# A three-stage audio tower kernel: new instruction orders, experts and gate output per 128 tokens, whole filter rows

## The chip, the cores and the metric

One NeuronCore of a Trainium2 chip runs the whole kernel. The metric is the device time in microseconds (us), lower is better. Engines: PE (TensorE), DVE (VectorE), ACT (ScalarE), POOL (GpSimd) and SP (SyncE, which here only issues DMAs). Each engine works through its own queue in order and meets the others through semaphores.

## The reference, cut to what matters

The input is 32 sequences of 750 rows of 256 channels. Each sequence becomes 3 segments of 128 tokens (every second row, zero-padded), that is T = 384 tokens. Per sequence:

```
h   = softmax(x x^T / 16) x                                 # per 128-token segment
z   = layernorm(h)
q,k,v = silu(causal_conv4(z W)) ; beta = sigmoid(z Wb)
o_delta = delta rule in chunks of 32 tokens, 4 heads of 64   # T = inv(I + A), state S over time
short, long = causal_conv3(v), causal_conv63(v)
w   = softmax(mlp([z, statistics of the four branches]))     # the gate, 4 weights per head
o   = rmsnorm(w0*short + w1*long + w2*o_delta + w3*v) Wo
h   = h + o
out = h + sum over the best 2 of 6 experts of layernorm(h)   # router, gelu MLPs 256 -> 128 -> 256
```

All is float32.

## The kernel before

Three stages run one after another; the loops are fully unrolled, each engine has its own hand-written list of calls, and the order of these lists is the schedule. NB = 32 sequences, BLK = 3 blocks of 128 tokens.

**First stage** (`first_phase`): attention, projections, the three-lag convolution of q, k and v, normalisation factors. Step i works on sequence a = i (attention), b = i-1 (projections and convolution taps), c = i-2 (short filter, k and v turned to tokens) and d = i-3 (masking of the k products). On DVE the 18 convolution taps of a sequence (`tap`, L737) are most of the work. `find_max` (L705) waits for PE's scores, `row_stats` (L716) for ACT's `divide_attn`, `variances` (L722) for the statistics just made. SP also writes one band of the long filter's Toeplitz tensor per issue (`expand`, 128 issues in all), 128 columns wide.

**Middle stage** (`second_phase`): the 63-tap filter as a matmul with Toeplitz tiles, 32 groups of 8 channels, four tile buffers. SP loads each group as two halves of 64 rows and 128 columns (64 issues, rows of 512 B), DVE clears the corner that the second half leaves empty, and PE does, per half group, four matmuls of 128 rows (L1050) and four of 64 rows (L1054) for what spills into the next 128-token block. Before groups 8, 16 and 24 stand three wide matmuls (`dense`, L1034). Meanwhile DVE inverts the 32x32 systems (`solve_column`, L1335 and L1338) and ACT stores the result of each head. The stage's last issues of SP are the first loads of the last stage.

**Last stage** (`third_phase`): step i works on n = i (products of q, k, kb; merging the inverses; state updates over the three blocks), it = i-1 (gate and mixture), e = i-2 (output projection, second norm, router, experts 0 to 2) and f = i-3 (experts 3 to 5). The names and lines that the prediction uses:

- PE: `products` L1468, `merge_a` to `merge_d` (L1477, L1488/L1491, L1499, L1507), `gate_out` L1587 (12 matmuls of the code, gate logits), `updates` L1538, `route` L1624, `state_update` L1547, `outputs` L1554, `kb_state` L1516, `q_state` L1524, `hidden` L1635, `expert_out` L1645 (all three blocks of an expert in one call).
- DVE: `mask` L1881 (masks the products; ACT's `copy_kk` then frees the bank), `gate_logits` L1943 to L1953, `gate_weights` L1958 to L1962, `weigh` L1968 and L1971, `state` L1917 (first) and L1919, routing L2017 to L2042, `remainder` L1908 (makes the right side R of the next `updates`), `add_expert` L2063.
- POOL: `VB` L2177, and, once the gate weights are there, L2182 and L2184 (two products of 768 columns per partition), and the powers of -1/2 (L2171, L2188).
- `solve_column` also runs here, on DVE: two columns in each of the steps 6 to 20, one to three in steps 0 to 5, after the second norm (`second_norm`, L2012) and before `gate_logits`.

A bank of PSUM that PE writes is read by DVE or ACT, and the next write waits for them. Most waits of PE in the last stage are of this kind.

## Time and profile before

| | us |
|---|---|
| median of 3 runs (lowest, highest) | 2646.76 (2645.16, 2649.2) |
| the profiled execution, its own time | 2644.78 |
| its span, first to last instruction | 2643.1 |
| PE, DVE, ACT, POOL busy | 2392.8, 1922.0, 1366.2, 562.4 |
| granted PE clock, mean | 0.966 |

The granted clock is given as a share of full speed: 1.00 is 2.4 GHz and 0.50 is 1.2 GHz. A row of the timeline has the start, the duration, engine, line, operation, what is written and read, a count of equal instructions in a row, and in brackets the engine's idle time before it with what ended it. An fp32 matmul of the code is two hardware matmuls, so x6 on L1645 are three matmuls of the code.

### The profile page before, as it was taken

To read this page: it belongs to the slowest core of one execution; us is meant where nothing else is said; L and a number is where in the kernel's file an instruction comes from. 1 tells how busy PE (TensorE), PEld (TensorE's weight loads), DVE (VectorE), ACT (ScalarE), POOL (GpSimd) and SP (SyncE) were. 2 spreads that over 40 slices of the span, in tenths; PEclk is the share of its full clock that TensorE was granted. 3 is DMA by queue.
4 is the path that set the end of the run, shared out by engine and by line. 5 is a ranking of instruction groups with operands and counts; after the bars stand their busy time and mean duration, and the time that the engine had idled before them with its cause. 6 is when DMAs were issued, how large, how long until landed. Compare 5 with 4: busy or idle time off the path is not lost.

```text
span 2643.1 us, 53850 instructions
## 1 busy us (share of the span) xinstructions
PE 2392.8 (91%) x21052; PEld 1789.0 (68%) x21052; DVE 1922.0 (73%) x5205; ACT 1366.2 (52%) x2633; POOL 562.4 (21%) x413
## 2 busy tenths in 40 slices
PE   5999999999698689999999999999999999999996
PEld 3666666666577567767777777777777777677764
DVE  3999999999684447676777677767775666657655
ACT  3888888887334144444444444444445444544442
POOL 1444444444200011111111111111111111111111
PEclk9999999999678589999999999999999999999999
DMA  2566666666889313221322122212322231223100
GB/s 85 202 218 224 214 212 225 216 214 214 209 218 282 110 58 112 67 70 64 108 100 70 64 94 90 70 64 76 108 70 88 70 114 65 70 70 111 64 19 19
DMA packets 253500, 318.25 MB, mean 120 GB/s; under 512 B 114496, under 2 KB 224032, under 8 KB 244544
## 3 DMA queue, kind: packets, MB, share of 16 engines
q1 hardware_dynamic: 248928, 292.78, 34.2%
q10 hardware_dynamic: 2304, 12.58, 1.4%
q0 software_dynamic: 2016, 9.44, 1.1%
q8 instruction: 169, 2.77, 0.4%
q14 instruction: 83, 0.68, 0.1%
HBM read 175.43 MB, written 156.11 MB: 125 GB/s over the span
## 4 chain that ended last, share of the span: by engine, by line
PE 41%; DVE 17%; ACT 6%; issue 3%; POOL 0%; DVEq 0%
PE bank L1645 7%; PE bank L1576 6%; PE bank L1635 5%; PE bank L1468 4%; PE bank L1587 4%; DVE DL L1977 3%; PE bank L1606 3%; ACT L1782 3%; DVE v_all L2063 3%; PE bank L1580 2%; PE bank L1499 2%; PE bank L1507 2%; PE bank L1554 1%; DVE e L2022 1%; ACT HE L1782 1%
## 5 line engine op out<-in xcount | busy, mean ns | idle before, releaser
L737 DVE SCALAR_TENSOR_TENSOR Y<-bank,convw,Y 128x383 f32<-128x383 f32 (+2 forms) x576 | 328.7, 603 | 4.5 <-ACT Y L626 3.2
L1645 PE MATMUL bank<-w2e,HE 128*128 128x256 f32 x1152 | 289.8, 388 | 12.1 <-DVE v_all L2063 9.2
L2063 DVE SCALAR_TENSOR_TENSOR v_all<-bank,we,v_all 128x256 f32<-128x256 f32 x576 | 242.8, 477 | 78.8 <-PE bank L1645 76.9
L1635 PE MATMUL bank<-v_all,w1e 128*128 128x384 f32 x768 | 285.9, 495 | 1.4 <-ACT HE L1782 1.4
L448 PE MATMUL bank<-pb,wqkv 128*128 128x384 f32 x768 | 275.3, 489 | 0.6 <-DVE Y L737 0.6
L1943 DVE TENSOR_TENSOR L<-bank,b2g 128x48 f32<-128x48 f32 x32 | 6.6, 207 | 344.0 <-PE bank L1587 344.0
L1645 PEld LDWEIGHTS bank<-w2e,HE 128*128 128x128 f32 x1152 | 208.1, 192 | 49.3 <-issue 16.6
L1576 PE MATMUL bank<-v_all,w1g 128*128 128x384 f32 x512 | 201.9, 518 | 0.4 <-ACT v_all L1774 0.4
L1782 ACT ACTIVATE HE<-bank 128x384 f32<-128x384 f32 x192 | 94.1, 490 | 194.8 <-PE bank L1635 194.1
L1765 ACT ACTIVATE v_all<-bank 128x192 f32<-128x192 f32 x192 | 60.1, 331 | 253.6 <-DVE v_all L1881 253.5
L2182 POOL TENSOR_TENSOR v_all<-v_all,WT 128x768 f32<-128x768 f32 x32 | 72.6, 2267 | 506.9 <-DVE WT L1962 506.9
L1635 PEld LDWEIGHTS bank<-v_all,w1e 128*128 128x128 f32 x768 | 134.1, 191 | 64.9 <-issue 9.6
L448 PEld LDWEIGHTS bank<-pb,wqkv 128*128 128x128 f32 x768 | 134.4, 191 | 61.4 <-issue 1.1
L2188 POOL TENSOR_TENSOR m<-m,minus_half_q 128x12 f32<-128x12 f32 x32 | 72.6, 2268 | 334.6 <-DVE m L1983 334.6
L626 ACT ACTIVATE Y<-bank,convw 128x384 f32<-128x384 f32 x192 | 111.5, 581 | 56.5 <-PE bank L448 54.1
L1757 ACT ACTIVATE first_stage<-bank 32x384 f32<-32x384 f32 (+1 forms) x192 | 89.0, 479 | 99.1 <-PE bank L1488 43.3
L1468 PE MATMUL bank<-v_all 64*128 64x256 f32 x768 | 115.1, 420 | 20.4 <-PEq L1009 14.4
L1554 PEld LDWEIGHTS bank<-W,v_all 128*128 128x128 f32 x768 | 98.4, 196 | 33.8 <-ACT W L1757 25.9
L1782 ACT ACT_TABLE_LOAD x93 | 119.3, 1283 | 1.7
L1554 PE MATMUL bank<-W,v_all 128*128 128x64 f32 x768 | 105.2, 281 | 15.1 <-ACT W L1757 15.1
L2171 POOL TENSOR_TENSOR b<-b,minus_half_q 128x3 f32<-128x3 f32 x32 | 27.1, 848 | 428.9 <-DVE b L2007 428.9
L1576 PEld LDWEIGHTS bank<-v_all,w1g 128*128 128x128 f32 x512 | 88.0, 191 | 42.8 <-issue 1.2
(213 smaller groups left out, 5440.9 us busy)
## 6 DMA issues: line engine op xcount, KB each, us to landing
packa<-pa SPq DMA_DIRECT2D x32, 1932.0 KB, 6.2
v_all<-packa SPq DMA_DIRECT2D x32, 1932.0 KB, 7.7
packb<-pb SPq DMA_DIRECT2D x32, 768.0 KB, 4.3
v_all<-packb SPq DMA_DIRECT2D x32, 768.0 KB, 7.0
toeplitz<-taps SPq DMA_DIRECT2D x128, 128.0 KB, 3.3
toep<-toeplitz SPq DMA_DIRECT2D x64, 256.0 KB, 7.1
packb<-fsk SPq DMA_DIRECT2D x32, 384.0 KB, 2.3
first_stage<-fl SPq DMA_DIRECT2D x32, 384.0 KB, 5.5
```

What stands on the lines that cost most here:

```text
L448: mm = pe.matmul(proj_bank[j][:, 0:T], wqkv[:, a, j * P:(j + 1) * P], xnT[:, a, :], start=(a == 0), stop=(a == HALF - 1), skip_group_check ...
L626: act.activation(Y[:, j, :], proj_bank[j][:, 0:T], ACT.Copy, scale=convw[:, j, CK - 1:CK])\
L737: dve.scalar_tensor_tensor(out=Y[:, j, lag:T], in0=proj_bank[j][:, 0:T - lag], scalar=convw[:, j, CK - 1 - lag:CK - lag], in1=Y[:, j, lag: ...
L1468: mm = pe.matmul(bank[odd][:, hh * 2 * P:(hh + 1) * 2 * P], kT[rows, hh, pair * P:(pair + 1) * P], qkb[rows, :, hh, pair * P:(pair + 1) * ...
L1554: mm = pe.matmul(bank[1][:, h * DH:(h + 1) * DH], ATM[:, even_heads_first(b, h), 0:P], W[:, h, :], start=(b == 0 and h == 0), stop=True, s ...
L1576: pe.matmul(mlp_bank[m][:, 0:T], w1g[:, a, m * P:(m + 1) * P], chans(pb[s], PX)[:, a, :], start=(a == 0), stop=False)
L1587: mm = pe.matmul(bank[4][:, b * P:(b + 1) * P], GH[:, m, b * P:(b + 1) * P], w2g[:, m, :].unsqueeze(1).broadcast_to([P, P // (4 * NH), 4 * ...
L1635: mm = pe.matmul(bank[6][:, 0:T], w1e[:, a, k, :], YT[s][:, a, :], start=(a == 0), stop=(a == HALF - 1))
L1645: mm = pe.matmul(expert_bank(b), HE[k % 2][:, b * P:(b + 1) * P], w2e[:, k, :], start=True, stop=True)
L1757: return act.activation(dst, src, ACT.Copy)
L1782: act.activation(HE[k % 2][:, :], bank[6][:, 0:T], ACT.Gelu_apprx_tanh).then_inc(he_ready.sem, 1)
L2063: dve.scalar_tensor_tensor(out=HA[s][:, b, :], in0=expert_bank(b), scalar=we[s][:, b, k:k + 1], in1=HA[s][:, b, :], op0=ALU.mult, op1=ALU. ...
```

## The change

- **Filter rows.** `toeplitz` is TW = 190 columns wide instead of 128. `expand` writes 190 columns, always from offset P-1-p. A group is loaded with one DMA of 128 whole rows (8 channels x 190 columns = 6080 B in a row), DVE's four clears of the corner and PE's wait for them go, and the second four matmuls take all 128 rows.
- **Experts per block.** `expert_out`, `add_expert`, `gate_out`, `input_stats`, the statistics of the delta branch and `second_norm` are called per block (or per pair of heads), so that other work can stand between. `eo_ready` counts 18 per sequence instead of 6. The third block's adds go on one by one; the first two share a bank and the first add waits for both.
- **Last stage, order.** Every engine has one `step(i)` as in the first stage, with another order. What is done is the same.
- **First stage, order.** PE, ACT, DVE and POOL lists are in another order, and so are the taps.

```diff
-            "toeplitz": nc.dram_tensor("toeplitz", [P, D, P], F32, kind="Internal").ap(),
+            "toeplitz": nc.dram_tensor("toeplitz", [P, D, TW], F32, kind="Internal").ap(),
...
-                    for half in range(2):
-                        rows = slice(half * DH, (half + 1) * DH)
-                        sp.dma_start(toep[it % NT][rows, :, half * (FL - 1):half * (FL - 1) + P],
-                                     dram["toeplitz"][rows, it * CG:(it + 1) * CG, :]).then_inc(toep_loaded[it % NT].sem, 16)
+                    sp.dma_start(toep[it % NT][:, :, :], dram["toeplitz"][:, it * CG:(it + 1) * CG, :])\
+                        .then_inc(toep_loaded[it % NT].sem, 16)
...
-                                mm = pe.matmul(acc[0:TW - P, o + NB:o + BLK * NB], toep[s][DH:P, ch, P:],
-                                               v_all[DH:P, it * CG + ch, 0:(BLK - 1) * NB],
+                                mm = pe.matmul(acc[0:TW - P, o + NB:o + BLK * NB], toep[s][:, ch, P:],
+                                               v_all[:, it * CG + ch, 0:(BLK - 1) * NB],
...
-                for s in range(NT):
-                    dve.memset(toep[s][DH:P, :, 0:FL - 1], 0.0).then_inc(setup, 1)
...
-                def expert_out(e, k):
+                def expert_out(e, k, b):
                     pe.wait_ge(*he_ready.now(e, k + 1))
...
+                    pe.wait_ge(*(acc_done.now(e, BLK * (k - 1) + max(b + 1, 2)) if k else acc_done.now(e - 1, BLK * (NE - 1) + max(b + 1, 2))))
+                    pe.matmul(expert_bank(b), HE[k % 2][:, b * P:(b + 1) * P], w2e[:, k, :], start=True, stop=True)\
+                        .then_inc(eo_ready.sem, 1)
...
+                def add_expert(e, k, b):
+                    s = e % 2
                     if k == 0:
                         dve.wait_ge(*we_step.now(e, 4))
...
+                    dve.wait_ge(*eo_ready.now(e, BLK * k + max(b + 1, 2)))
...
# DVE, last stage, around the masks
+                    if 0 <= n < NB:
+                        mask(n, 3)
+                        solve_columns(n)
                         mask(n, 4)
                         mask(n, 5)
...
# DVE, first stage, the end of a step
+                    if 0 <= a < NB:
                         row_stats(a, 0)
...
                         row_stats(a, 1)
...
                         row_stats(a, 2)
-                        variances(a)
                     if 0 <= c < NB:
                         copy_kbT(c)
-                    if 0 <= b < NB:
+                    if 0 <= a < NB:
+                        variances(a)
...
+                        tap(b, 3, 3)
                         tap(b, 4, 1)
+                    if 0 <= a < NB:
+                        normalise(a, 0)
+                        normalise(a, 1)
```

**Place 1: DVE in the last stage, from the gate weights to the remainder.** `m` stands for the small tiles m12, s12 and r12, `c` for cmp and eqs, `e` and `g` for the router's small tiles; first_stage is where the state S lies. Before:

```order
L1962 TENSOR_TENSOR WT<-WT,m 128x48
L1968 TENSOR_TENSOR DL<-DL,WT 128x768
L1917 COPY first_stage<-bank 64x2x64 x2
L2017 TENSOR_TENSOR c<-e,anchors 128x108
L2020 TENSOR_REDUCE e<-c 128x18
L2022 SCALAR_TENSOR_TENSOR e<-e,rclip 128x18
L2029 TENSOR_TENSOR c<-e 128x108
L2030 TENSOR_TENSOR c<-e 128x108
L2031 TENSOR_REDUCE g<-e 128x3
L2033 TENSOR_TENSOR c<-c,before_e 128x108
L2035 TENSOR_TENSOR e<-e,g 128x18
```

After:

```order
L1966 TENSOR_TENSOR WT<-WT,m 128x48
L2020 TENSOR_TENSOR c<-e,anchors 128x108
L2023 TENSOR_REDUCE e<-c 128x18
L2025 SCALAR_TENSOR_TENSOR e<-e,rclip 128x18
L1972 TENSOR_TENSOR DL<-DL,WT 128x768
L2033 TENSOR_TENSOR c<-e 128x108
L2034 TENSOR_TENSOR c<-e 128x108
L2035 TENSOR_REDUCE g<-e 128x3
L2037 TENSOR_TENSOR c<-c,before_e 128x108
L2039 TENSOR_TENSOR e<-e,g 128x18
L1922 COPY first_stage<-bank 64x2x64 x2
```

The copy of the first state, second after the gate weights before, now stands behind the eight router instructions.

**Place 2: PE in the last stage, from the gate output to the second block's updates.** Before:

```order
L1587 MATMUL bank<-w2g,v_all 128x128 x12
L1538 MATMUL bank<-VB,first_stage 128x128 x3
L1538 MATMUL bank<-VB,first_stage 128x64
L1645 MATMUL bank<-w2e,HE 128x256 x3
L1624 MATMUL bank<-router,v_all 128x126 x6
L1547 MATMUL bank<-W,v_all 128x128 x2
L1635 MATMUL bank<-v_all,w1e 128x384 x2
L1554 MATMUL bank<-W,v_all 128x64 x4
L1635 MATMUL bank<-v_all,w1e 128x384 x2
L1516 MATMUL bank<-first_stage,v_all 128x128 x2
L1645 MATMUL bank<-w2e,HE 128x256 x3
L1538 MATMUL bank<-R,first_stage 128x128 x3
```

After:

```order
L1565 MATMUL bank<-w2g,v_all 128x128 x12
L1605 MATMUL bank<-router,v_all 128x126 x6
L1516 MATMUL bank<-VB,first_stage 128x128 x3
L1516 MATMUL bank<-VB,first_stage 128x64
L1616 MATMUL bank<-v_all,w1e 128x384 x2
L1525 MATMUL bank<-W,v_all 128x128 x2
L1532 MATMUL bank<-W,v_all 128x64 x4
L1622 MATMUL bank<-w2e,HE 128x256
L1492 MATMUL bank<-first_stage,v_all 128x128 x2
L1616 MATMUL bank<-v_all,w1e 128x384 x2
L1622 MATMUL bank<-w2e,HE 128x256
L1516 MATMUL bank<-R,first_stage 128x128 x3
```

The reader of the first state (L1516 before, L1492 after) had two `hidden` and one whole `expert_out` ahead of it since the gate output, and has one `hidden` and one block of `expert_out` now; a `hidden` and a block follow it, ahead of the updates that need R.

**Place 3: DVE in the last stage, around the solve columns** (step of columns 15 and 16 after, 11 and 12 before). Before:

```order
L2012 TENSOR_SCALAR v_all<-v_all,bmv,b 128x256 x3
L1335 TENSOR_TENSOR prod<-X 128x660
L1338 TENSOR_TENSOR X<-X,prod 128x3x11x20
L1335 TENSOR_TENSOR prod<-X 128x684
L1338 TENSOR_TENSOR X<-X,prod 128x3x12x19
L1943 TENSOR_TENSOR L<-bank,b2g 128x48
```

After:

```order
L1886 TENSOR_TENSOR v_all<-bank,upper 128x2x128
L1332 TENSOR_TENSOR prod<-X 128x720
L1335 TENSOR_TENSOR X<-X,prod 128x3x15x16
L1332 TENSOR_TENSOR prod<-X 128x720
L1335 TENSOR_TENSOR X<-X,prod 128x3x16x15
L1886 TENSOR_TENSOR v_all<-bank,upper 128x2x128 x2
```

The columns have moved from behind the second norm to between the fourth mask and the last two.

## Rows read from the trace of the kernel before

**Rows 1.** By stretch: length, PE, PEld, DVE, ACT, POOL busy, PEclk, DMA share, GB/s.
```profile
400.00:419.80 19.80, 18.27 (x215) 13.08 (x214) 19.26 (x52) 16.14 (x36) 8.73 (x8) 1.00 0.63 218
697.00:867.00 170.00, 145.85 (x1042) 125.05 (x1042) 110.15 (x168) 60.51 (x75) 5.92 (x11) 0.75 0.96 246
703.80:748.00 44.20, 44.20 (x222) 38.07 (x223) 38.31 (x54) 11.73 (x14) 3.23 (x6) 0.50 0.82 187
973.50:2520.00 1546.50, 1464.61 (x11986) 1101.05 (x11986) 1072.60 (x3082) 716.16 (x1305) 245.94 (x144) 1.00 0.24 81
```
**Rows 2.** Waits of PE in 973.5 to 2520: total, times, longest.
```profile
PE bank L1538 <- DVE R L1908: 30.1, 29, 1.1
PE bank L1516 <- DVE first_stage L1919: 22.8, 29, 0.8
```
**Rows 3.** Timeline of PE, one step of the last stage.
```profile
1732.51 1.00 PE L1538 MATMUL bank<-VB,first_stage 128*128 128x128 f32 x8
1733.35 1.51 PE L1645 MATMUL bank<-w2e,HE 128*128 128x256 f32 x6
1734.70 1.50 PE L1624 MATMUL bank<-router,v_all 128*128 128x126 f32 x12
...
1738.61 1.51 PE L1635 MATMUL bank<-v_all,w1e 128*128 128x384 f32 x4
...
1740.40 1.46 PE L1645 MATMUL bank<-w2e,HE 128*128 128x256 f32 x6
1742.93 1.08 PE L1538 MATMUL bank<-R,first_stage 128*128 128x128 f32 x8 [1.07 <-DVE R L1908]
```
**Rows 4.** Timeline of DVE, the same step.
```profile
1732.71 0.21 DVE L1943 TENSOR_TENSOR L<-bank,b2g 128x48 f32<-128x48 f32 x1 [8.46 <-PE bank L1587]
...
1736.08 0.20 DVE L1958 TENSOR_REDUCE m<-WT 128x12 f32<-128x48 f32 x1
...
1736.82 0.96 DVE L1968 TENSOR_TENSOR DL<-DL,WT 128x768 f32<-128x768 f32 x1
1737.69 0.58 DVE L1917 COPY first_stage<-bank 64x128 f32<-64x128 f32 x2
1738.31 0.95 DVE L2017 TENSOR_TENSOR c<-e,anchors 128x108 f32<-128x108 f32 x1
...
1739.59 1.05 DVE L2022 SCALAR_TENSOR_TENSOR e<-e,rclip 128x18 f32<-128x18 f32 x1
1740.68 0.27 DVE L2029 TENSOR_TENSOR c<-e 128x108 f32<-128x108 f32 x1
...
1741.55 0.27 DVE L2038 TENSOR_TENSOR c<-c 128x108 f32<-128x108 f32 x1
```
**Rows 5.** Timeline of POOL, the same step.
```profile
1736.86 2.27 POOL L2182 TENSOR_TENSOR v_all<-v_all,WT 128x768 f32<-128x768 f32 x1 [14.91 <-DVE WT L1962]
1739.09 1.52 POOL L2184 TENSOR_TENSOR v_all<-v_all,WT 128x768 f32<-128x768 f32 x1
```
**Rows 6.** One line's instructions: ns shortest/median/longest, first and last start.
```profile
L2022 DVE SCALAR_TENSOR_TENSOR e<-e,rclip x32: 178/1053/1057, 992.2 to 2617.1; 128x18 f32<-128x18 f32 x32
```
**Rows 7.** Timeline of DVE, the second of two solve columns.
```profile
1562.46 0.91 DVE L1335 TENSOR_TENSOR prod<-X 128x720 f32<-128x720 f32 x1
```
**Rows 8.** DMA queues in 697 to 867: packets, MB, share of 16 engines.
```profile
q1 hardware_dynamic: 40143, 20.53, 59.7%
q10 hardware_dynamic: 2304, 12.58, 21.2%
```
**Rows 9.** Timeline of DVE, first stage.
```profile
402.29 0.56 DVE L705 TENSOR_REDUCE s<-bank 128x3 f32<-128x384 f32 x1 [0.17 <-PE bank L417]
...
410.03 0.31 DVE L722 BATCH_NORM_AGGREGATE mv<-st 128x2 f32<-128x6 f32 x3
```
**Rows 10.** Timeline of PE near the end, after an idle stretch.
```profile
2611.06 0.85 PE L1615 MATMUL bank<-ident,v_all 128*128 128x128 f32 x6 [2.50 <-DVE v_all L2012]
2611.74 2.63 PE L1645 MATMUL bank<-w2e,HE 128*128 128x256 f32 x6
```

More of the change, by code:

```diff
@@ new lines, in step @@
+                    if 0 <= n < NB:
+                        updates(n, n % 2, 0)
+                    if 0 <= e < NB:
+                        hidden(e, e % 2, 0)
+                    if 0 <= n < NB:
+                        state_update(n, n % 2, 0)
+                        outputs(n, 0)
+                    if 0 <= f < NB:
+                        expert_out(f, 5, 2)
+                    if 0 <= n < NB:
+                        kb_state(n, n % 2, 1)
+                    if 0 <= e < NB:
+                        hidden(e, e % 2, 1)
+                        expert_out(e, 0, 0)
@@ L1754, in _ @@
+                for i in range(NB + 3):
+                    step(i)
             @block.scalar
@@ L1872, in _ @@
-                body(it=NB - 1, e=NB - 2, f=NB - 3, s=1)
-                body(e=NB - 1, f=NB - 2, s=0)
-                body(f=NB - 1, s=1)
+                for i in range(NB + 3):
+                    step(i)
             @block.vector
@@ L2099, in body @@
[L2099 to L2109 removed]
+                    if 0 <= e < NB:
+                        residual(e, e % 2)
@@ L2200 @@
+                for i in range(NB + 2):
+                    step(i)
 _ATTN = ["Wq", "Wk", "Wv", "Wb", "conv_q_w", "conv_k_w", "conv_v_w", "fir_short_w", "fir_long_w", "mlp_w1", "mlp_b1",
```

832 lines of the change are left out of this document (425 added, 407 removed).

## Prediction, made before the changed kernel was run

> **What bounds the kernel now.** I read the busy time by stretch first [rows 1]. In the first stage DVE is busy 19.26 of 19.80 us, a whole step: DVE sets the pace there. In the middle stage (697 to 867) the DMA engines are busy for 0.96 of the time and PE's granted clock is 0.75; from 703.8 to 748 it is 0.50, and there PE is busy throughout while the DMA share is 0.82, so in that part PE is the bound and elsewhere DMA is. In the last stage PE is busy 1464.6 of 1546.5 us at clock 1.00; over its 29 steps of 53.4 us that leaves 81.9 / 29 = 2.8 us idle a step. The waits of PE say where [rows 2]: the right side R (1.1 a step) and the state S (0.8), both from DVE; the other 0.9 is two copies by ACT. The gain of an order lies in these 2.8 us, since no order takes away work.
>
> **Last stage, steady steps.** A wait costs more than its idle time: six matmuls of `expert_out` take 1.35 us to the next start (1733.35 to 1734.70) and 2.53 (1740.40 to 1742.93) with the 1.07 us wait behind them [rows 3], so about 0.1 more. Four waits are 2.8 + 4 x 0.15 = 3.4 us. Splitting `expert_out` adds no matmul. In the new PE order a block or a `hidden` stands in each of the four places, so these waits go. What is late next? I followed the new order from the end of `gate_out` at 1732.51, with the durations of before.
>
> PE reaches `kb_state` (it needs the first new state) after `route`, `state_update`, `hidden` and `outputs`, together 3.91 (1734.70 to 1738.61), `updates` 0.84 (1732.51 to 1733.35) and one block of `expert_out` 0.45 (a third of 1.35) [rows 3]: at 1737.7.
>
> DVE starts the gate logits at 1732.71; four operations of 0.24 and ACT's exp of the same 48 columns, taken as one more (an estimate), end at 1733.94; the weights take 0.74 (1736.08 to 1736.82) [rows 4]: 1734.68. Before, `weigh` and the copy of the state followed at once. Now the router's three operations stand first. Here the trace shows something that the order does not: L2022 works on 18 columns and lasts 1.05 us in the median but 0.18 at its shortest [rows 6], and the long ones end with POOL's second product: 1739.59 + 1.05 = 1740.64 against 1739.09 + 1.52 = 1740.61 [rows 4, 5]. L2017, 0.95 us, ends just past the first product's end, 1739.13, while L2029 on the same 108 columns takes 0.27. So a DVE operation with two inputs in SBUF stands still while POOL reads for its product, and POOL's product in turn ends 1.35 us after the DVE operation that got in first: 1739.13 - 1737.78 behind L1968, 1740.61 - 1739.26 behind L2017 [rows 4, 5].
>
> In the new order: L2017's operation gets in first (as L1968 did, 0.04 us ahead of POOL), 0.27, to 1734.95; POOL's first product ends 1.35 later, 1736.30; the operation of L2022 waits for it and ends at 1736.35; the second product ends 1.35 later, 1737.70; `weigh`, 0.96, two inputs in SBUF, waits for that, and is let in some 0.1 before its end: 1738.5; the ranking, 0.87 (1740.68 to 1741.55), 1739.4; the two state copies, 0.58, 1740.0. PE starts `kb_state` at 1740.1 instead of 1737.7: one wait of 2.4 us in the place of four that cost 3.4. Behind it, followed call by call in the same way, R, the second state and the experts' sums come 0.5 us or more ahead of PE. 29 x (3.4 - 2.4) = 29 us saved. With nothing standing still the copies would be ready at 1734.95 + 0.33 + 0.2 + 0.9 + 0.87 + 0.58 = 1737.8, and the wait 0.2: 93 us saved. I take the first, since all but the last of the 32 executions of L2022 fit it.
>
> The Trainium skill, page "SBUF — State Buffer", section "Who interferes with whom", has the rule: a VectorE instruction with two SBUF inputs and a GpSimd instruction that reads SBUF exclude each other for the whole instruction. It speaks against this order, which puts two such operations and then `weigh` where POOL works. By it the saving is the 29 us, without it 93; the 1.05 against 0.18 us above agree with it.
>
> **Last stage, the solve columns.** Before, they run while DVE waits for the gate output, with 8.46 us of idle left behind them [rows 4]: they cost nothing. Now they stand ahead of the last two masks, and `merge_a` on PE waits for ACT's copies behind these masks: queued behind it are the gate's matmuls and all the rest of the step. An operation on 720 columns takes 0.91 [rows 7], a pair of columns up to 4 x 0.94 = 3.8 us. The margin is bounded by nothing below and by 3.8 above; I estimate 1.8 (about 1.4 in which the fifth mask would wait for PE's third products anyway, and 0.4 of PE's `hidden`). By size (0.2 us an operation and 1 us for each 960 columns) the pairs of steps 6 to 20 take 1.35, 2.0, 2.55, 3.0, 3.35, 3.6, 3.75, 3.8 and back; what is over 1.8 adds to 17 us lost (0 to 43 at the ends). Steps 0 to 2 have two or three columns and little else to do: 4 us more lost, less if PE's wait for the residual in step 2 goes.
>
> **Middle stage.** Queue 10 stores 6144 B in a row per partition: 21.2% of 16 x 170 us for 12.58 MB, 46 engine-us per MB. Queue 1: 59.7% is 1624 engine-us for 20.53 MB; 58 half groups of 256 KB are 15.2 MB, the other 5.3 MB at 46 take 244, so 512 B rows cost 1380 / 15.2 = 91 per MB [rows 8]. The new group is 778 KB in pieces of 6080 B, nearest to queue 10: 29 x 0.778 = 22.6 MB x 46 = 1040. That saves 340 / 16 = 21 us where DMA is the bound, which it is in 126 of 170 us [rows 1]: 16, and I take 14, since a faster feed leaves PE's half-clock part as it is. The ends are 22 and, if the rows cost what 512 B rows cost, 42 lost. The four cleared corners and PE's wait for them cost nothing before. The first stage writes half as much again of Toeplitz rows; its DMA share of 0.63 [rows 1] covers that.
>
> The Trainium skill, page "DMA: Bandwidth & Descriptors", table "Specifications", gives 512 B as the transfer from which the line rate is reached. By that rule the new rows bring only the larger volume: this is a rival below. The 91 against 46 above speak against it.
>
> **First stage.** DVE is the bound, so only its own gaps count. Where nothing is waited for, an operation starts 0.08 us before the last one's end. `find_max` starts 0.17 after it, 0.25 lost; it now has three more DVE operations ahead of it since the copy of x, and PE makes the scores half a projection earlier. `variances` starts at 410.03, 0.10 behind the statistics that it needs [rows 9], 0.18 lost; a copy now stands between. Two taps of one tile in a row (0.11) are parted. That is 0.54 a step; the three `row_stats` in a row may wait 0.1 for ACT. 31 x 0.45 = 14 us saved, with 20 saved and 10 lost as ends.
>
> **Sum**, against the profiled execution's 2644.8: -29 + 17 + 4 - 14 - 14 = -36, 2609; the median of the runs is 2 above: **2611 us**.
>
> **Rivals.** *No standing still* (the copy of the state comes in time): 64 us more saved, 2547. For it: the new order fits exactly if each operation lasts its undisturbed time. Against it: rows 5 and 6. 15%. *The clock falls*, the one that ends slower: at 2611.06 PE had been idle for 2.50 us, and the next `expert_out`, six matmuls, took 2.63 instead of 1.46 [rows 3, 10]: 1.2 us, about 2 with what follows. The new wait is 2.4 us long, in one piece, before `hidden`; the four of before are at most 1.1. If the clock falls behind it in every step, 58 us more: 2669. It turns the result from 18 steps on (36 / 2). Against it: 2.4 is the shorter idle time. 15%. *Wide rows bring only bytes*: 7.4 MB more at 46 and DMA-bound for 126 of 170 us is 16 us lost where I count 14 won: 2641. 5%. *The middle stage is held by PE at half clock*: nothing won there, 2625. 10%. *The first stage gains a wait* of 1 us a step, since all its lists are new: 31 more and no 14: 2656. 5%.
>
> **How the numbers follow.** The forecast has 50%, with 2580 to 2640 as its own range from the ends of the margin (1 to 3 us) and of the middle stage. The range 2565 to 2655 leaves out most of the first rival and half of the second, about 2 in 10. A change under 0.2% (5.3 us) can't be told from none. Faster by more (below 2641.5): the forecast, the first and fourth rival, half of the third and part of the clock rival, 0.82; within: 0.06; slower: 0.12.
>
> **What the profile after would show.** PE waiting at `kb_state` for DVE's first state, 2.2 to 2.4 us a step, no wait at `updates` for R; L2025 (L2022 before) and `weigh` long, ending with POOL's products; in steps 7 to 19 PE waiting before `merge_a` for ACT, up to 2 us, and periods that rise and fall with the columns: 52.4 without columns, up to 54.4 with them; the toep queue's engine time down by a fifth and the middle stage 10 to 20 us shorter; DVE's period in the first stage 19.3. It would be wrong most of all if PE's clock drops behind the new wait, or if the state copies come in time.

## The result and the profile after

| | before | after |
|---|---|---|
| median (lowest to highest), us | 2646.57 (2645.16 to 2649.2, 4 runs) | 2534.92 (2528.05 to 2547.43, 4 runs) |
| profiled execution, its span | 2643.1 | 2526.3 |
| granted PE clock, mean | 0.966 | 0.978 |

The ratio is 0.9582, with a 95% interval from 0.9536 to 0.9628. The forecast was 2611 us with a range of 2565 to 2655: the direction was right, the gain is three times the size forecast, and the time lies outside the range. A second series gave 2537.97 against 2647.26, 0.9591 (0.9569 to 0.9613).

I cut the spans at the same places of the program and compared each part with its term in the sum. The profiled execution of the kernel after was the fastest of its four: the spans differ by 116.8 us, the medians by 111.7.

| part | before, us | after, us | difference | forecast |
|---|---|---|---|---|
| start to the first dense matmul | 689.9 | 671.8 | -18.1 | -14 |
| middle stage, to the first product of the last stage | 177.4 | 140.8 | -36.6 | -14 |
| filling, products of sequences 0 to 2 | 139.8 | 138.1 | -1.7 | +4 |
| 28 steady steps (products 3 to 31) | 1494.5 | 1446.9 | -47.6 | -12 (-29 and +17) |
| from the last products to the end | 141.5 | 128.7 | -12.8 | none |

The sum is -116.8. Two terms were far too small, and one was missing. Below, the period is the time from the first product of one sequence to that of the next. The stretches of the profile after, with the columns of [rows 1] (length, PE, PEld, DVE, ACT, POOL busy, PEclk, DMA share, GB/s): a step of the first stage, the middle stage, the steady part of the last.

```profile
382.00:401.27 19.27, 18.04 (x214) 12.98 (x214) 19.10 (x51) 15.95 (x36) 8.72 (x8) 1.00 0.72 237
671.80:812.60 140.80, 119.74 (x1052) 101.83 (x1053) 110.35 (x175) 60.89 (x75) 7.86 (x15) 0.94 0.96 365
927.00:2402.00 1475.00, 1414.84 (x11676) 1079.98 (x11677) 1055.81 (x3035) 713.67 (x1284) 239.66 (x143) 1.00 0.25 84
```

The DMA share of the middle stage is 0.96 as before, but it moves 365 GB/s where it moved 246, and PE's clock is 0.94 where it was 0.75 [rows 1]; it falls only at 798.8 us, behind the last filter matmul (795.3). PE's waits in 973.5 to 2380, against the list in [rows 2]:

```profile
PE bank L1492 <- DVE first_stage L1922: 50.1, 27, 1.9
```

Of the four waits a step one is left, at `kb_state` (L1492), for the first state copy: the place that the forecast named. PE, DVE and POOL around it (against [rows 3 to 5]):

```profile
1864.48 1.50 PE L1605 MATMUL bank<-router,v_all 128*128 128x126 f32 x12
...
1869.29 0.65 PE L1622 MATMUL bank<-w2e,HE 128*128 128x256 f32 x2
1871.80 0.71 PE L1492 MATMUL bank<-first_stage,v_all 128*128 128x128 f32 x4 [1.86 <-DVE first_stage L1922]
```
```profile
1866.42 0.21 DVE L1966 TENSOR_TENSOR WT<-WT,m 128x48 f32<-128x48 f32 x1
1866.55 0.27 DVE L2020 TENSOR_TENSOR c<-e,anchors 128x108 f32<-128x108 f32 x1
1866.85 0.27 DVE L2023 TENSOR_REDUCE e<-c 128x18 f32<-128x108 f32 x1
1867.15 1.09 DVE L2025 SCALAR_TENSOR_TENSOR e<-e,rclip 128x18 f32<-128x18 f32 x1
1868.16 0.94 DVE L1972 TENSOR_TENSOR DL<-DL,WT 128x768 f32<-128x768 f32 x1
1869.03 1.56 DVE L2033 TENSOR_TENSOR c<-e 128x108 f32<-128x108 f32 x1
...
1871.16 0.58 DVE L1922 COPY first_stage<-bank 64x128 f32<-64x128 f32 x2
```
```profile
1866.71 1.50 POOL L2231 TENSOR_TENSOR v_all<-v_all,WT 128x768 f32<-128x768 f32 x1 [11.84 <-DVE WT L1966]
1868.17 2.30 POOL L2236 TENSOR_TENSOR v_all<-v_all,WT 128x768 f32<-128x768 f32 x1
```

Read them together. L2025, 18 columns and two inputs, lasts 1.09 us and ends with POOL's first product; L2023, which has one input, takes its 0.27 us while that product runs. `weigh` (L1972) starts at 1868.16, 0.01 us ahead of POOL's second product, and runs its 0.94 undisturbed; the product ends 1.4 us after it, at 1870.47, and L2033, 108 columns, stands for 1.56 us until then.

### The profile page after: what moved, and what is told of

It reads as the page before. It is cut to its first block, busy times and chain, and to the rows that moved or that the text cites. A ratio compares the mean times of both kernels' runs of the same rounds, so it can differ in the third digit from the quotient of the medians.

```text
span 2526.3 us, 54742 instructions
## 1 busy us (share of the span) xinstructions
PE 2317.6 (92%) x21052; PEld 1750.0 (69%) x21052; DVE 1909.3 (76%) x5201; ACT 1369.0 (54%) x2633; POOL 555.4 (22%) x413
## 3 DMA queue, kind: packets, MB, share of 16 engines
q1 hardware_dynamic: 219744, 309.03, 36.6%
## 4 chain that ended last, share of the span: by engine, by line
PE 49%; DVE 14%; issue 2%; ACT 2%; POOL 1%; DVEq 0%
PE bank L1622 8%; PE bank L1616 7%; PE bank L1555 6%; PE bank L1559 4%; PE bank L1565 3%; PE bank L1442 3%; PE bank L1585 2%; PE bank L1475 2%; PE bank L1483 2%; PE bank L1516 2%; PE bank L1532 2%; DVE c L2033 2%; DVE v_all L2069 2%; PE bank L1492 1%; DVE e L2025 1%
## 5 line engine op out<-in xcount | busy, mean ns | idle before, releaser
L2069 DVE SCALAR_TENSOR_TENSOR v_all<-bank,we,v_all 128x256 f32<-128x256 f32 x576 | 263.4, 478 | 287.5 <-PE bank L1622 285.1
L1622 PE MATMUL bank<-w2e,HE 128*128 128x256 f32 x1152 | 328.9, 391 | 7.2 <-DVE v_all L2069 4.2
L1616 PE MATMUL bank<-v_all,w1e 128*128 128x384 f32 x768 | 289.0, 499 | 1.1 <-ACT HE L1758 0.8
L448 PE MATMUL bank<-pb,wqkv 128*128 128x384 f32 x768 | 282.3, 491 | 1.8 <-DVE Y L738 1.8
L1555 PE MATMUL bank<-v_all,w1g 128*128 128x384 f32 x512 | 187.3, 489 | 0.0
L1616 PEld LDWEIGHTS bank<-v_all,w1e 128*128 128x128 f32 x768 | 131.9, 191 | 63.9 <-issue 10.4
L1753 ACT ACTIVATE v_all<-bank,b1g 128x384 f32<-128x384 f32 x128 | 74.4, 581 | 147.1 <-PE bank L1559 145.9
L2231 POOL TENSOR_TENSOR v_all<-v_all,WT 128x768 f32<-128x768 f32 x32 | 48.7, 1522 | 405.9 <-DVE WT L1966 405.9
L1555 PEld LDWEIGHTS bank<-v_all,w1g 128*128 128x128 f32 x512 | 95.2, 191 | 53.3 <-issue 0.6
L1559 PE MATMUL bank<-first_stage,w1s 128*128 128x384 f32 x256 | 113.1, 523 | 1.4 <-ACT first_stage L1736 1.4
L1886 DVE TENSOR_TENSOR v_all<-bank,upper 128x256 f32<-128x256 f32 x192 | 73.7, 412 | 51.7 <-PE bank L1442 51.5
L1442 PEld LDWEIGHTS bank<-v_all 64*128 64x128 f32 x768 | 69.3, 194 | 61.5 <-issue 46.8
```

Source lines behind the costliest of these rows:

```text
L448: mm = pe.matmul(proj_bank[j][:, 0:T], wqkv[:, a, j * P:(j + 1) * P], xnT[:, a, :], start=(a == 0), stop=(a == HALF - 1), skip_group_check ...
L1442: mm = pe.matmul(bank[odd][:, hh * 2 * P:(hh + 1) * 2 * P], kT[rows, hh, pair * P:(pair + 1) * P], qkb[rows, :, hh, pair * P:(pair + 1) * ...
L1555: pe.matmul(mlp_bank[m][:, 0:T], w1g[:, a, m * P:(m + 1) * P], chans(pb[s], PX)[:, a, :], start=(a == 0), stop=False)
L1559: pe.matmul(mlp_bank[m][:, 0:T], w1s[:, m * P:(m + 1) * P], SGT[:, :], start=False, stop=True)\
L1616: mm = pe.matmul(bank[6][:, 0:T], w1e[:, a, k, :], YT[s][:, a, :], start=(a == 0), stop=(a == HALF - 1))
L1622: pe.matmul(expert_bank(b), HE[k % 2][:, b * P:(b + 1) * P], w2e[:, k, :], start=True, stop=True)\
```

## The experiments

**The standing still.** GpSimd's products are cut short: the first as shown, the second (L2236) in the same way.

```diff
+                    m = NM if it < 2 else 1
-                    pool.tensor_tensor(ta..., heads(pb[it % 2], PF), WT[:, :, 0:1]..., ALU.mult)
+                    pool.tensor_tensor(ta[..., 0:m, :], heads(pb[it % 2], PF)[:, 0:m, :], WT[:, 0:m, 0:1]..., ALU.mult)
...
-                        mix_add(it, it % 2, 1, ta[:, :].rearrange("p (m d) -> p m d", d=DH))
+                        mix_add(it, it % 2, 1, DL[it % 2][:, :, :])
```

> The kernel after with GpSimd's two products of 768 columns a partition cut to 64 columns from the third sequence on; the sum that takes the first product reads the delta branch twice in its place. So the filter and value branches of the mixture are left out, and DVE and PE do the same instructions as in the kernel after. Theory 1, a DVE operation with two inputs in SBUF and a GpSimd product shut each other out: the third routing operation lasts 0.18 us, no longer 1.09, and the first of the ranking 0.27, no longer 1.56, so the state copies end 2.2 us earlier, ahead of PE, the wait of 1.86 us at the state product goes and the period falls from 51.2 to about 49.0 us. Rival, the long operations wait for something else (a semaphore, ACT): they stay long and the period stays 51.2 us.

The time was 2478.09 us (one run), although PE's clock fell in the middle stage, which took 157.3 us. The steady period is 49.08 us, and 49.3 to 50.1 in the steps of products 9 to 17 (the solve columns), and the wait at the state product is gone. L2025 and L2033 of the kernel after, then of this one (ns shortest, median, longest; the first two sequences still have the whole products):

```profile
L2025 DVE SCALAR_TENSOR_TENSOR e<-e,rclip x32: 178/1094/1099, 932.2 to 2504.3; 128x18 f32<-128x18 f32 x32
L2033 DVE TENSOR_TENSOR c<-e x32: 270/1556/1559, 934.1 to 2504.5; 128x108 f32<-128x108 f32 x32
```
```profile
L2025 DVE SCALAR_TENSOR_TENSOR e<-e,rclip x32: 177/178/1094, 951.6 to 2454.4; 128x18 f32<-128x18 f32 x32
L2033 DVE TENSOR_TENSOR c<-e x32: 260/263/1555, 953.5 to 2454.6; 128x108 f32<-128x108 f32 x32
```

DVE's instructions are the same, so it is POOL's products that make these two operations long, and the rival falls: they put 0.92 + 1.29 = 2.21 us on DVE's way to the state copy. The Trainium skill, page "SBUF — State Buffer", section "Who interferes with whom", has this rule, and the two medians agree with it.

The period of 49.08 us is worth more than the theory. It is a step with the same matmuls in which PE shows no wait worth the name. In the order of the kernel after, the wait costs 51.20 - 49.08 = 2.12 us a step, where 1.86 are seen as idle time. The step of before is 53.36 - 49.08 = 4.28 us longer, where 2.8 were seen and 3.4 was my term; as its order is another one, not all of the 4.28 need be waits.

**The first state copy earlier.**

```diff
                         routing_logits(e)
+                    if 0 <= n < NB:
+                        state(n, 0)
                     if 0 <= it < NB:
                         weigh(it, it % 2, 2)
...
                         rank_routes(e)
                     if 0 <= n < NB:
-                        state(n, 0)
                         delta_out(n, n % 2, 0)
```

> The kernel after with the copy of the first new state moved from behind the ranking to behind the three operations of the routing logits, ahead of the weighing of the delta branch. Theory 1: the 1.86 us in which PE waits at the state product come from the weighing and the ranking ahead of that copy and from their standing still beside GpSimd's two products. The state product of PE would find its state ready (the copies end 0.6 us after the state update, some 0.7 us before PE comes to it). A wait costs PE about 0.3 to 0.4 us more than its idle time (four waits became one, and the rest of the step fell by 1.21), so the period goes from 51.2 to about 49.0, if nothing else is late; the remainder R may come 0 to 0.9 us late, as it has weighing, ranking and the first filter on its way: 49.0 to 50.2, and 30 to 64 us saved in all. Rival, the order only trades one wait for another of the same size: a wait of 1.5 us or more at the update products and a period above 50.8.

Measured: 2518.25 us (2510.51 to 2522.08), ratio 0.9519 (0.9498 to 0.954), period 50.62. The wait at the state product went and two shorter ones came:

```profile
PE bank L1516 <- DVE R L1913: 22.0, 27, 0.8
PE bank L1500 <- DVE DL L1930: 6.2, 28, 0.3
```

The period is 0.4 above the range of theory 1 and below the bound of its rival; the gain, 17 us by the medians, is about half of the least that was expected (30). The remainder did come 0.81 us late, the upper end of what was allowed, and the second wait, for the delta output that PE's state query overwrites, was not foreseen.

**The solve columns moved back.**

```diff
                         mask(n, 3)
-                        solve_columns(n)
                         mask(n, 4)
...
                         second_norm(e, 2)
                     if 0 <= n < NB:
+                        solve_columns(n)
                         input_stats(n, 4)
```

> The kernel after with the solve columns moved back behind the second norm, ahead of the statistics of the fifth pair of heads, where DVE has 8.2 us of idle time before the gate logits. Theory 1: the periods of steps 9 to 17, 51.5 to 53.9 us in place of 51.2, come from the columns ahead of the fifth and sixth mask; all are 51.2 here and 13 us are saved in the last stage. Rival: the periods rise with the number of columns wherever they stand, since DVE is that much busier in the step; then they stay at 52 to 54 us.

Measured: 2526.52 us (2515.04 to 2528.16), ratio 0.9539 (0.9513 to 0.9566); the lowest is 13.0 below the lowest of the kernel after. All steady periods are 51.2 (one is 51.27). In the kernel after the periods of products 9 to 17 were 51.49, 53.48, 52.13, 53.89, 53.91, 52.20, 53.72, 51.82 and 51.45: together 13.3 us above 51.20. Theory 1 is shown. Part of the 13.3 is the clock: in four of these steps, and in no other steady step, it fell after the 1.86 us wait. One of them, the stretch and PE's timeline:

```profile
1348.40:1351.80 3.40, 3.40 (x10) 2.29 (x9) 3.37 (x6) 0.50 (x2) 0.00 (x0) 0.50 0.23 77
```
```profile
1347.41 0.71 PE L1492 MATMUL bank<-first_stage,v_all 128*128 128x128 f32 x4 [1.86 <-DVE first_stage L1922]
1347.96 2.34 PE L1616 MATMUL bank<-v_all,w1e 128*128 128x384 f32 x4
```

L1616 takes 1.46 us for four matmuls at full clock and 2.34 here. Where the 1.86 us wait is absent, in the kernel with the state copy earlier, the columns cost 6.8 us in all and the clock never falls there.

**The experts in one piece.** The order of the kernel after, but on PE the three blocks of each expert stand together again, at the place of the first.

```diff
                     if 0 <= f < NB:
                         hidden(f, f % 2, 4)
                         expert_out(f, 3, 0)
                         expert_out(f, 3, 1)
+                        expert_out(f, 3, 2)
                     if 0 <= n < NB:
                         products(n, n % 2, 1)
-                    if 0 <= f < NB:
-                        expert_out(f, 3, 2)
...
```

> The kernel after with the three blocks of each expert's second product called in one piece on PE, each at the place of its first block; the order of everything else and DVE's adds stay as they are. Theory 1: the split by itself gives little in the steady steps, since one more block of 0.45 us stands ahead of the gate output and one less behind it: the wait at the state product grows from 1.86 to 2.3 us and the period from 51.2 to 51.6; the last 130 us, in which little else is left to do, lose 5 to 10 us, since PE waits for the adds of a whole expert. Together 15 to 25 us more than the kernel after at the same clock. Rival: the split is what carries the gain, the waits of before come back in the order's place, and the period is 52.5 us or more.

Measured: 2636.65 us (one run), periods from 53.8 to 56.7, the last part 134.6 us. The rival was right and my 51.6 far off: with whole experts at these places the new order's periods are longer than the 53.36 us of the kernel before, and the last stage takes 1822.6 us in place of 1775.8 before and 1713.7 after. PE's waits in 1000 to 2380, and what follows the longest:

```profile
PE bank L1492 <- DVE first_stage L1914: 58.5, 25, 2.3
PE bank L1622 <- DVE v_all L2061: 11.2, 25, 0.5
PE bank L1559 <- ACT first_stage L1728: 11.0, 25, 0.6
PE bank L1516 <- DVE R L1905: 4.0, 25, 0.2
```
```profile
1487.01 1.22 PE L1492 MATMUL bank<-first_stage,v_all 128*128 128x128 f32 x4 [2.34 <-DVE first_stage L1914]
1488.02 2.57 PE L1616 MATMUL bank<-v_all,w1e 128*128 128x384 f32 x4
```

The wait has the 2.3 us expected. What I left out is three more waits, 1.05 us a step, and the clock: it was at 0.50 for 3.4 to 7 us in 22 places of the steady part, where the kernel after has 4. L1492 takes 1.22 in place of 0.71, L1616 2.57 in place of 1.46. This is the forecast's second rival. That the forecast's own wait of 2.4 us would have met it too is an argument, not shown; the kernel after, with 1.86 us, met it in four steps. Whole experts at other places were not tried, so what the split is worth in the best order of each kind is open.

**The whole rows alone, in the kernel before.**

```diff
-            "toeplitz": nc.dram_tensor("toeplitz", [P, D, P], F32, kind="Internal").ap(),
+            "toeplitz": nc.dram_tensor("toeplitz", [P, D, TW], F32, kind="Internal").ap(),
...
-                    for half in range(2):
-                        rows = slice(half * DH, (half + 1) * DH)
-                        sp.dma_start(toep[it % NT][rows, :, half * (FL - 1):half * (FL - 1) + P], ...
+                    sp.dma_start(toep[it % NT][:, :, :], dram["toeplitz"][:, it * CG:(it + 1) * CG, :])\
+                        .then_inc(toep_loaded[it % NT].sem, 16)
...
```

> The kernel before with the whole filter rows alone: TW = 190 columns written and loaded, one load per group, no cleared corner, all 128 rows in the second matmuls. Nothing else differs. The middle stage, from the first dense matmul to the first product of the last stage, took 177.3 us before and 140.8 after. Theory 1, engine time: what the DMA engines have to do fell from 0.96 x 16 x 177.3 = 2723 to 0.96 x 16 x 140.8 = 2163 engine-us, and that alone sets the stage; here too it is 139 to 143 us, with queue 1 near 57% of 16 engines, and the whole kernel 35 to 38 us below the time before. Theory 2, the forecast as written: 14 us saved, 160 to 166 us, with PE's granted clock at 0.50 for some 40 us or more of it. Theory 3: the order of the first stage, not the rows, kept the clock up; then the clock falls here as before and the stage is 155 us or more.

Measured: 2614.22 us (one run), middle stage 146.9 us. That is 30.5 us less, between the theories: theory 1's engine time is there, but the clock fell once, behind a wait of 2.27 us for the rows, and then PE was the bound. The whole stage and that stretch:

```profile
689.30:836.20 146.90, 138.04 (x1052) 117.89 (x1053) 110.37 (x175) 61.09 (x75) 7.86 (x15) 0.84 0.90 331
761.80:802.70 40.90, 40.90 (x211) 35.79 (x210) 38.86 (x63) 18.29 (x23) 1.99 (x4) 0.50 0.74 265
```

**What makes the rows cheap.** Three variants of the kernel after: the tile padded, so that pieces are 760 B; each group as two loads of 64 partitions; both. The edits:

```diff
-        toep = [sb(f"toep{s}", [P, CG, TW]) for s in range(NT)]
+        toep = [sb(f"toep{s}", [P, CG, TW + 2]) for s in range(NT)]
...
-                    sp.dma_start(toep[it % NT][:, :, :], dram["toeplitz"][:, it * CG:(it + 1) * CG, :])\
+                    sp.dma_start(toep[it % NT][:, :, 0:TW], dram["toeplitz"][:, it * CG:(it + 1) * CG, :])\
...
-                                mm = pe.matmul(acc[0:TW - P, o + NB:o + BLK * NB], toep[s][:, ch, P:],
+                                mm = pe.matmul(acc[0:TW - P, o + NB:o + BLK * NB], toep[s][:, ch, P:TW],
```
```diff
-                    sp.dma_start(toep[it % NT][:, :, :], dram["toeplitz"][:, it * CG:(it + 1) * CG, :])\
...
+                    for half in range(2):
+                        rows = slice(half * DH, (half + 1) * DH)
+                        sp.dma_start(toep[it % NT][rows, :, :], dram["toeplitz"][rows, it * CG:(it + 1) * CG, :])\
```

> The kernel after with the tile of the filter rows padded from 190 to 192 columns a channel, so that a row lands in pieces of 760 B and no longer of 6080 B. The bytes, the number of loads and PE's work are the same. Theory 1, a price per piece: 512 B cost 91 engine-us per MB before and 6080 B about 43 now, that is 0.0466 and 0.264 us a piece; a line through both gives 0.056 us for 760 B, 74 per MB, so 24.9 MB cost 1840 instead of 1080 engine-us. The middle stage gets 760 / 16 = 47 us longer, about 188 us. Theory 2, one load in place of two half loads is what brought the gain: the stage stays at 141 us. Theory 3, PE's clock: the stage is longer only where the granted clock is 0.50. Under theory 1 queues 0 and 10, whose bytes are unchanged, would go back from 41 and 38 engine-us per MB to 49 and 46 if pieces of different queues wait for each other, and stay if they don't.

> The kernel after with each group of filter rows loaded as two DMAs of 64 partitions, as before the change, but still in pieces of 6080 B. What the DMA engines spend: before, pieces of 512 B in half loads cost 91 engine-us per MB; whole loads cost 43 in pieces of 6080 B and, by the run with the padded tile, about 50 to 55 in pieces of 760 B. So a price per piece alone doesn't fit. Theory 1, the half load of 64 partitions is what made the rows of before dear: here queue 1 takes 60 engine-us per MB or more for these rows and the middle stage is 155 us or longer even at full clock. Theory 2, the short piece is, with a jump between 512 and 760 B: here 43 to 46 per MB, and the stage as in the kernel after, 141 us without and 157 us with a fall of PE's clock.

> The kernel after with half loads of 64 partitions and the tile padded to 192 columns, so pieces of 760 B: the same number of pieces of each load as before the change, each half as long again. Theory 1, half loads are dear: 80 to 90 engine-us per MB, a middle stage of 180 us or more. Theory 2, a jump between 512 and 760 B: 50 to 55 per MB as with whole loads, and a stage of 155 to 160 us. Theory 3, both together (few partitions and short pieces): between the two, and then the run with half loads of 6080 B shows nothing.

The whole kernels took 2549.6, 2564.3 and 2579.9 us, one run each. Queue 1 in the middle stage of before, after, padded, half loads, both (packets, MB, share of 16 engines), one fence each:

```profile
q1 hardware_dynamic: 41278, 21.07, 58.6%
```
```profile
q1 hardware_dynamic: 12123, 29.20, 56.9%
```
```profile
q1 hardware_dynamic: 39992, 29.10, 61.9%
```
```profile
q1 hardware_dynamic: 11872, 29.10, 64.0%
```
```profile
q1 hardware_dynamic: 40544, 29.10, 74.2%
```

An engine-us is a microsecond of one of the 16 DMA engines. The share times 16 times the stage's length, less some 190 engine-us for the 4.3 MB that are not filter rows (45 per MB, an estimate from queue 10's 46 in [rows 8]), over 16.8 MB before and 24.9 MB in the others:

| loads, pieces | middle stage, us | engine-us per MB of filter rows |
|---|---|---|
| before: half, 512 B | 177.4 | 88 |
| half, 760 B | 186.5 | 81 |
| half, 6080 B | 173.9 | 64 |
| whole, 760 B | 157.5 | 55 |
| whole, 6080 B (after) | 140.8 | 44 |

Theory 1 of the padded run, a price per piece, falls: it wanted 74 per MB and 188 us. Queues 0 and 10 did not go back either (42 and 40 per MB in the padded run, 53 and 43 with half loads of 6080 B). The two runs with half loads came out as the first theory of each. What the runs don't part: a half load has 64 partitions, but also half the bytes, and there are twice as many; and a piece of 760 B is shorter than 6080 B, but it also begins every 768 B in the tile. The half load is the dearer half of the matter: at the same piece it costs 20 to 26 per MB, the short piece 11 to 17. My forecast put the whole difference down to the length of the rows, and was right in the sum (46 against 44) only because the change mends both. The Trainium skill, page "DMA: Bandwidth & Descriptors", section "Rules for kernel authors", advises one transfer of 128 partitions in place of two to disjoint halves, since the two serialize; these runs go further, as here they cost 64 against 44. My third rival, wide rows that bring only bytes, is refuted by a stage that is 36.6 us shorter; that a longer piece still pays above 512 B is what 55 against 44 for whole loads says, from one run of the padded tile.

The stage's lengths hold clock falls too (granted mean 0.80 in the padded run, 0.74 and 0.73 with half loads), so they can't be read as DMA alone. The price per MB moves less: in two runs with whole loads of 6080 B and one fall of the clock (the whole rows alone, and the kernel with the solve columns moved back) it comes to 46 where it is 44 without a fall. In the runs with half loads PE waited longer for rows, 3.31 us at the first place and up to 6.5, and the clock fell at each wait of over 3 us.

**The clock in the middle stage.** The kernel with the solve columns moved back has the same middle stage as the kernel after, yet took 156.9 us for it. The place where they part, the kernel after first:

```profile
741.24 1.13 PE L1049 MATMUL bank<-v_all,toep 128*128 128x96 f32 x8 [1.52 <-DMA toep<-toeplitz]
742.30 0.67 PE L1053 MATMUL bank<-v_all,toep 128*62 128x64 f32 x8
```
```profile
743.36 1.85 PE L1049 MATMUL bank<-v_all,toep 128*128 128x96 f32 x8 [2.19 <-DMA toep<-toeplitz]
745.14 1.11 PE L1053 MATMUL bank<-v_all,toep 128*62 128x64 f32 x8
```
```profile
743.60:787.90 44.30, 44.30 (x228) 38.91 (x228) 42.16 (x66) 18.69 (x23) 2.18 (x4) 0.50 0.76 273
```

After 1.52 us of idle time PE goes on at full clock, after 2.19 at half, for 44 us, in which the DMA share is 0.76: there PE is the bound. It costs 156.9 - 140.8 = 16 us. The length of the wait does not decide alone: in the kernel with the state copy earlier 2.11 us at this place left the clock at 1.00 (141.6 us), and in the kernel with GpSimd's short products it fell behind 2.28 us (157.3 us). Two runs ask whether the scatter of the kernel after comes from here, the first of the kernel unchanged, the second with this edit:

```diff
                         if it and it % GI == 0:
                             dense(3)
+                        if it == 17:
+                            dense(2)
```

> The kernel after once more, unchanged. Its times lie at 2528 and at 2542 to 2547 us. Theory: the two groups are the middle stage without and with a fall of PE's granted clock behind the wait of 1.5 to 2.2 us for the 18th group of filter rows (140.8 to 141.6 us without, 156.9 with, in kernels whose middle stage is the same); so the times stay in these two groups, and the profile shows either a middle stage of 141 us and a time near 2528, or 157 us and a time near 2543. Rival: the slower times come from other places (the waits of 1.86 us in the last stage, where the clock fell for 3.4 us in 4 of 30 steps); then the middle stage is 141 us in a slow run too.

> The kernel after with two wide matmuls, some 1.7 us, ahead of the 18th group of filter rows, where PE waits 1.5 to 2.2 us for the rows. They write banks that nobody reads then. Theory 1, the fall of the clock follows on that wait: it is now 0 to 0.6 us, the clock stays at 1.00, the middle stage is 141 us in every run and the times are 2526 to 2532 us. Rival 1, the wait moves on: the DMA engines are as busy as before, PE waits 2 us at a later group and the clock falls there, so the times are in two groups as in the kernel after. Rival 2, the matmuls cost what they last: 142 to 143 us and nothing else.

The kernel after: 2532.71 (profiled, middle stage 143.2 us at clock 1.00), 2535.64, 2540.31 and 2540.54. Two groups were expected; there is no clean split, the times of both series lie all over the stretch from 2528 to 2547. With two wide matmuls at that place: 2526.85 to 2530.36 in five runs, 2528.3 in the median, and a wait of 0.41 us where 1.5 to 2.2 were. The middle stage is 140.8 us, so the matmuls cost nothing that shows. The scatter of the kernel after over both series is 19.4 us (7.8 in the second alone), with them 3.5. The mean granted clock of whole executions fits: 0.965 to 0.969 in the five of the kernel after above 2535 us, 0.975 to 0.978 in the three below, 0.973 to 0.979 in the five with the matmuls; one fall of 44 us to half makes 22 / 2530 = 0.009. So it is likely that most of the scatter comes from this wait; a profile of one of the longer executions of the kernel after, which would show the fall, was not taken.

**All edits together.**

```diff
# on DVE, beside the state copy, the solve columns and dense(2) as above
                         delta_out(n, n % 2, 0)
-                    if 0 <= e < NB:
-                        keep_best(e)
-                    if 0 <= n < NB:
                         remainder(n, 1)
+                    if 0 <= e < NB:
+                        keep_best(e)
...
+                    if 0 <= n < NB:
+                        delta_out(n, n % 2, 1)
                     if 0 <= it < NB:
                         dve.wait_ge(*vw_ready.now(it))
                         mix_add(it, it % 2, 4, tb[:, :].rearrange("p (m d) -> p m d", d=DH))
-                    if 0 <= n < NB:
-                        delta_out(n, n % 2, 1)
```

> The kernel after with four edits together: the solve columns behind the second norm, the first state copy behind the routing logits, the remainder R ahead of the first filter of the routes and the delta output of the second block ahead of the last sum of the mixture, and the two wide matmuls ahead of the 18th group. Expected from the single runs: the waits at the state product (1.86) and at the update products (0.81) and the state query (0.22) go; the shortest step seen, with GpSimd's products cut, has 49.08 us; here 49.1 to 49.7, no rise of the periods with the columns. From 2510.5, the best time with the state copy alone, 28 x (50.62 - 49.4) = 34 and 7 for the columns: 2469 us, and 2485 where the clock falls in the middle stage. Rival: the weighing, now behind the state copy, still stands still beside GpSimd's second product and makes R or the weighted sums late: 50 us or more and 2490 to 2500.

Measured: 2494.16 us (2489.0 to 2496.99), ratio to the kernel before 0.9426 (0.9405 to 0.9447), against 0.9591 (0.9569 to 0.9613) for the kernel after in the same series. It beats both. The period is 50.49 and flat (one is 50.71), so the rival's numbers came true, its reason only in part: `weigh` stands still for 0.25 us (1.20 in the median, 0.95 in the kernel after), and R shows no idle time, but `updates` starts 0.29 us late. PE's waits in 1000 to 2370:

```profile
PE bank L1624 <- DVE v_all L2071: 11.0, 54, 0.4
```

Only 0.4 us a step are seen as idle, yet the period is 1.4 above 49.08. Measured from start to start, `expert_out` takes 0.38 us more a step than in the kernel with short products, `q_state` 0.27, `hidden` 0.16 and `updates` 0.08. I read these as waits that the modelled ends of the matmuls hide, as the matmuls are the same. Of the waits that are seen, the experts' adds, behind the longer row of the router and the mixture, are now the late ones.

## Why the forecast failed, step by step

- **The wait at the state copy: right in place and mechanism, 0.54 too long.** Forecast 2.4 us, measured 1.86. Counted from the end of the gate output, PE is ready at 5.46 us (forecast 5.19) and the copies end at 7.26 (forecast 7.5). I let POOL's second product in ahead of `weigh`; `weigh` got in first by 0.01 us, and the first operation of the ranking stood in its place. The time of the copies hardly changes by that. The error of 0.54 is made of two of about 0.25. But this wait too costs more than its idle time, 2.12 in all, which I had not added: net 0.28 us a step, 8 us over 28 steps.
- **What the four waits of before cost: the term that was mis-sized.** I took 2.8 + 4 x 0.15 = 3.4; the step is 4.28 shorter without waits and in the new order. The rows give 0.11 for the one wait that I looked at; I rounded up to 0.15 and took it for all, and gave the new wait none. Where the order stays the same, one wait costs 2.12 - 1.86 = 0.26 beyond its idle time, and the two waits of the kernel with the state copy earlier cost 50.62 - 49.08 - 1.03 = 0.51. Four at 0.26 with their idle time would be 3.8. The other 0.4 or so is not taken apart: `q_state` took 1.30 us a step before and 0.89 after, from start to start and without the idle time shown, so waiting is hidden in it, and the two orders differ in other places too. Together the term was 0.88 us a step too small, 25 us. With the first point the steady saving is 28 x (53.36 - 51.20) = 60.5 us where 29 was forecast; the 47.6 measured are this less the columns.
- **The solve columns: a number inside the range, in part by luck.** Forecast 17 us lost (0 to 43), measured 13.3. The columns alone cost 6.8 us in the kernel with the state copy earlier, so the margin ahead of `merge_a` was wider than the 1.8 us that I took; PE stands idle there in seven steps, 0.8 us at most, where I had said up to 2. The other half is the clock, which I had not reckoned with there. The 4 us in the filling seem right (133.9 us with the columns moved back, 138.1 in the kernel after), but the filling as a whole became 1.7 us shorter, and why was not looked into.
- **The middle stage: the step "a faster feed leaves PE's half-clock part as it is" failed.** The price of the new rows was right (46 forecast, 44 measured). But the half-clock part was itself a result of the slow feed. Before, PE stood 2.16, 3.84 and 3.37 us for rows, and each time the clock fell:

```profile
702.65 0.35 PE L1050 MATMUL bank<-v_all,toep 128*128 128x96 f32 x1 [2.16 <-DMA toep<-toeplitz]
```

  With the new feed the longest such wait is 1.52 us and the clock stays. With one fall the stage is 146.9 to 157.3 us in the kernels with the new rows, with none 140.8 to 143.2. I also counted the gain for queue 1 alone: queues 0 and 10, with unchanged bytes, fell from 48 and 46 to 41 and 38 engine-us per MB, together 160 engine-us or 10 us of the stage.
- **The end of the last stage: a missing term.** It is 12.8 us shorter and stood in no part of my sum. With the experts in one piece on PE 5.9 of the 12.8 are gone, some of them by the clock (PE's was at half for 10 us there). The rest comes from the order or from DVE's adds per block, which no run parts. The longest wait of PE, some 85 us into this part, fell from 4.55 us to 2.89, and from an expert's adds to ACT's `HE`; it is 2.89 us with the experts in one piece too, so it isn't PE's split that shortened it. The first line is of before, the second of after:

```profile
2591.60 0.77 PE L1645 MATMUL bank<-w2e,HE 128*128 128x256 f32 x1 [4.55 <-DVE v_all L2063]
```
```profile
2479.22 0.67 PE L1622 MATMUL bank<-w2e,HE 128*128 128x256 f32 x2 [2.89 <-ACT HE L1758]
```

- **The first stage: right.** The period is 19.20 where it was 19.78, 0.58 less; I had counted 0.54 and taken 0.45. `find_max` follows the operation ahead of it without idle time, where [rows 9] has 0.17:

```profile
391.91 0.55 DVE L706 TENSOR_REDUCE s<-bank 128x3 f32<-128x384 f32 x1
```

- **The rivals.** The clock rival was no fancy: it shows in the run with the experts in one piece at 2.34 us, and in four steps at 1.86. "No standing still" gave 2547, near the measured time for a wrong reason: the standing still is there in full. The run without it took 2478, with a fall of the clock in its middle stage.

## What to carry to other kernels

What a wait costs is not its idle time: take it from two periods, one with and one without the wait, and look for the same instructions with a longer distance from start to start. Where a slow clock follows on waits, the clock is part of what the feed costs, and a change to the feed moves both; so ask for each fall what PE had waited for, and put cheap matmuls where the wait can't be removed (two of them took the longer times away here). In a pipeline that runs dry at the end, cost the last steps as a part of their own.

## What the runs showed of the hardware that was not expected

- Two loads of 64 partitions took 64 engine-us per MB, one of 128 partitions 44, with the same rows of 6080 B. The reason was not looked for.
- Queues 0 and 10, whose own transfers did not change, became 16% cheaper per MB (48 to 41 and 46 to 38). With half loads of 6080 B on queue 1 they are at 53 and 43, with half loads of 760 B at 50 and 43, with whole loads of 760 B at 42 and 40: they go with the half loads of queue 1, not with the length of its pieces.
- The same idle time of PE may or may not be followed by half clock: in the middle stage 1.78 and 2.11 us were not, 2.16 to 2.28 were in four kernels, and in the padded run 1.41 us was, for 3.4 us; 1.86 us in the last stage was in 4 steps and wasn't in the others.
